# Moving the weight folds, one context split and one normalisation in a cross-attention kernel

## The reference

```
Q = (x @ Wq), K = (ctx @ Wk), V = (ctx @ Wv)      # x: 8 x 256 x 256, ctx: 8 x 256 x 192
score = Q K^T / sqrt(256), masked by mask_BxS2_if1
attn  = softmax(score)                            # 8 heads of width 256
out   = (attn V) @ Wo + x
return (out - mean(out)) * rsqrt(var(out) + 1e-5) * gamma + beta
```

## Time and profile before

| | |
|---|---|
| time, median of 3 | 321.18 us (321.13 to 321.34) |
| time of the profiled execution | 321.24 us |
| its span | 319.4 us |
| PE busy | 309.8 us (97%) |
| DVE, ACT, POOL busy | 253.2, 222.2, 181.0 us |
| granted TensorE clock | 0.998 of full speed |

### The profile page before, as it was taken

One profiled execution on the slowest core, in us unless ns is written; L12 is line 12 of the kernel. 1 busy time (PEld: TensorE's weight loads), 2 busy tenths in 40 slices (PEclk: granted clock), 3 DMA queues, 4 the chain that ended last, 5 costly groups with the idle time before them and its releaser, 6 DMA issues.

```text
span 319.4 us, 7403 instructions
## 1 busy us (share of the span) xinstructions
PE 309.8 (97%) x2264; PEld 290.2 (91%) x2264; DVE 253.2 (79%) x721; ACT 222.2 (70%) x601; POOL 181.0 (57%) x183
## 2 busy tenths in 40 slices
PE   8899998999999999999999999999999999999992
PEld 6898877999999999999999999999999999999982
DVE  0367768777999879987998879987998889975785
ACT  2446677677877787678776887678767887777640
POOL 1123259555864587457864586458755686457211
PEclk9999999999999999999999999999999999999999
DMA  7995444454345653474445454464355445440100
GB/s 257 366 406 213 135 131 129 126 182 136 130 150 166 207 163 113 158 209 168 131 123 179 165 164 143 140 218 149 114 188 163 170 117 182 141 145 13 35 33 33
DMA packets 46910, 50.26 MB, mean 157 GB/s; under 512 B 3504, under 2 KB 37040, under 8 KB 46896
## 3 DMA queue, kind: packets, MB, share of 16 engines
q1 hardware_dynamic: 46608, 49.56, 46.4%
q10 hardware_dynamic: 288, 0.52, 0.6%
HBM read 32.24 MB, written 17.83 MB: 157 GB/s over the span
## 4 chain that ended last, share of the span: by engine, by line
PE 89%; DVE 3%; POOL 2%; DMA 2%; ACT 1%; issue 1%; SPq 1%; POOLq 0%; DVEq 0%
PE score_bank L314 24%; PE out_bank L314 18%; PE gL_bank L314 13%; PE tL_bank L314 12%; PE tU_bank L314 8%; PE gU_bank L314 7%; DMA wq_raw<-in_wqT 2%; PE tL_bank L348 1%; PE spare_bank L348 1%; PE tL_bank L330 1%; PE tU_bank L330 1%; POOL pT_lo L1018 1%; DVE tU L817 1%; PE tU_bank L354 1%; PE spare_bank L314 1%
## 5 line engine op out<-in xcount | busy, mean ns | idle before, releaser
L995 POOL TENSOR_TENSOR probs<-probs,inv_sum 128x512 f32<-128x512 f32 x64 | 66.6, 1042 | 84.5 <-DVE inv_sum L780 83.9
L592 ACT ACTIVATE probs<-neg_scores,neg_max 128x256 f32<-128x256 f32 x128 | 64.2, 502 | 34.7 <-DVE neg_max L769 34.6
L1018 POOL TENSOR_TENSOR pT_lo<-pT_raw,pT_hi 128x512 fp32r<-128x512 f32 x60 | 76.5, 1296 | 11.7 <-ACT pT_hi L549 11.7
L769 DVE CUSTOM_DVE_ANT_0 neg_scores<-score_bank,mask_bias 128x256 f32<-128x256 f32 x128 | 49.1, 421 | 7.4 <-PE score_bank L314 4.6
L790 DVE STREAM_TRANSPOSE squares<-probs 128x512 f32<-128x512 f32 x60 | 42.3, 706 | 0.8 <-DMA scratch<-squares 0.3
L549 ACT ACTIVATE tL_hi<-tL_bank 128x512 fp32r<-128x512 f32 x31 | 18.5, 598 | 30.9 <-PE tL_bank L314 30.9
L314 PE MATMUL score_bank<-ctxT_hi,gU 128*128 128x256 f32 x128 | 36.6, 286 | 0.7 <-POOL ctxT_lo L1007 0.7
L314 PE MATMUL score_bank<-ctxT_hi,gL_lo 128*128 128x256 f32 x128 | 36.3, 284 | 0.0
L314 PE MATMUL score_bank<-ctxT_lo,gL_hi 128*128 128x256 f32 x128 | 36.3, 283 | 0.0
L314 PE MATMUL score_bank<-ctxT_hi,gL_hi 128*128 128x256 f32 x128 | 36.3, 283 | 0.0
L314 PE MATMUL score_bank<-ctxT_lo,gU 128*128 128x256 f32 x128 | 36.2, 283 | 0.0
(11 more groups left out here) (166 smaller groups left out, 946.4 us busy)
## 6 DMA issues: line engine op xcount, KB each, us to landing
scratch<-squares SPq DMA_DIRECT2D x30, 512.0 KB, 2.8
pT_raw<-scratch SPq DMA_DIRECT2D x120, 128.0 KB, 3.1
xT_raw<-in_xT SPq DMA_DIRECT2D x8, 256.0 KB, 4.5
ctxT_raw<-in_ctxT SPq DMA_DIRECT2D x8, 256.0 KB, 4.7
wo_raw<-in_wo SPq DMA_DIRECT2D x4, 512.0 KB, 13.4
x_res<-in_x SPq DMA_DIRECT2D x8, 256.0 KB, 3.2
out<-y_out SPq DMA_DIRECT2D x7, 256.0 KB, 2.7
wq_raw<-in_wqT SPq DMA_DIRECT2D x3, 512.0 KB, 7.9
```

The lines of the kernel that those rows point to most:

```text
L592: nc.scalar.activation(probs[j % 2][:, n, :], neg_scores[:, n, :], ACT.Exp, bias=neg_max[:, n:n + 1], scale=-1.0, accum_out=row_sum[:, n:n ...
L769: nc.vector.tensor_tensor_reduce(out=neg_scores[:, n, :], in0=score_bank[hh][:, q, :], in1=mask_bias[:], scale=-SCALE, scalar=3.0e38, op0= ...
L995: nc.gpsimd.tensor_tensor(probs[j % 2][:, rows, :], probs[j % 2][:, rows, :], inv, ALU.mult) \
L1018: nc.gpsimd.tensor_tensor(pT_lo[j % 2][:, k].rearrange("p hh (q i r) -> p (hh q) i r", q=QT, i=ROWS), pT_raw[j % 2][:, k].rearrange("p i n ...
```

## The change

1. **Folds of C.** Pair t is folded in step t, for t = 0 to 3. On PE a fold now stands ahead of `context_products`, so in step 3 pair 3 is folded ahead of the context products of step 0. The banks become spare/out for pairs 0 and 3 and tL/tU for pairs 1 and 2, on all three engines (`fold_C_banks`); pair 2 waits for the split of pair 1, pair 3 for that of pair 0. Context products of step 0 wait for the splits of three pairs, output products of step 0 for all four.
2. **ACT.** `C_hi_part` moves behind `pT_hi_part` within its step.
3. **Context of batch 0.** `ctx_hi_part(0)` and `ctx_lo_part(0)` move from step 3 to step 1, on ACT behind the query parts, on POOL behind `normalise_probs`.
4. **DVE.** `C_lo_part` stays at the end of the step: pairs 0 to 3 in steps 0 to 3. The wait for gamma and beta moves from ahead of step 3 to ahead of step 4.
5. **Tail.** `normalise(B - 2)` moves behind the last split. Batch 7 is normalised into `y_last`, which is `neg_scores`, and DVE no longer waits for the store of batch 6 there.

```diff
+        y_last = neg_scores[:, 0:QT, :]
+        def fold_C_banks(j):
+            n = (0, 1, 1, 0)[j]
+            return fold_banks[2 * n], fold_banks[2 * n + 1]
...
-                sp.dma_start(out[B - 1][:, q, :], y_out[:, q, :]).then_inc(out_stored, 16)
+                sp.dma_start(out[B - 1][:, q, :], y_last[:, q, :]).then_inc(out_stored, 16)
...
@@ fold_C (PE) @@
-                    pe.wait_ge(C_split, 2 * (j - 2) + 2)
-                lower, upper = fold_banks[2 * (j % 2)], fold_banks[2 * (j % 2) + 1]
+                    pe.wait_ge(C_split, 2 * (PAIRS - 1 - j) + 2)
+                lower, upper = fold_C_banks(j)
...
@@ context_products (PE), j == 0 @@
-                    pe.wait_ge(C_split, 2 * PAIRS)
+                    pe.wait_ge(C_split, 2 * (PAIRS - 1))
...
@@ output_lower (PE) @@
+                if j == 0:
+                    pe.wait_ge(C_split, 2 * PAIRS)
...
@@ step (PE) @@
+                for pair in folds:
+                    fold_C(pair)
                 if not (isinstance(t, int) and t < LAG):
                     context_products(t - LAG, jb, bb)
-                for pair in folds:
-                    fold_C(pair)
...
@@ all engines with folds (PE, ACT, DVE) @@
-            step(0, 0, 0, folds=[0])
-            step(1, 1, 0, folds=[1])
-            step(2, 2, 0, folds=[2, 3])
-            for t in range(LAG, PAIRS + 2):
+            for t in range(PAIRS):
+                step(t, t, 0, folds=[t])
+            for t in range(PAIRS, PAIRS + 2):
...
@@ step (ACT) @@
-                if j == PAIRS - 1:
+                if j == PAIRS - 1 and not (isinstance(t, int) and t < PAIRS):
                     ctx_hi_part(b)
...
+                if isinstance(t, int) and t == 1:
+                    ctx_hi_part(b)
+                if not (isinstance(t, int) and t < LAG - 1):
+                    pT_hi_part(t - LAG + 1, (j - LAG + 1) % PAIRS)
                 for pair in folds:
                     C_hi_part(pair)
-                if not (isinstance(t, int) and t < LAG - 1):
-                    pT_hi_part(t - LAG + 1, (j - LAG + 1) % PAIRS)
...
@@ step (POOL) @@
-                if j == PAIRS - 1:
+                if j == PAIRS - 1 and not (isinstance(t, int) and t < PAIRS):
                     ctx_lo_part(b)
                 normalise_probs(t, j)
+                if isinstance(t, int) and t == 1:
+                    ctx_lo_part(b)
...
@@ tail (DVE) @@
             centre(B - 2)
-            normalise(B - 2)
             t_lo_part_lower(STEPS - 2)
             tU_sum(STEPS - 2)
             t_lo_part_upper(STEPS - 2)
             tU_sum(STEPS - 1)
             t_lo_part_lower(STEPS - 1)
             t_lo_part_upper(STEPS - 1)
+            normalise(B - 2)
...
-            dve.wait_ge(out_stored, 16 * B)
             for q in range(QT):
                 dve.wait_ge(rstd_done, B + q)
-                normalise_tile(B - 1, q)
+                normalise_tile(B - 1, q, y_last)
```

More of the change, by code:

```diff
@@ L846, in centre_tile, with normalise_tile @@
                     ALU.subtract, ALU.mult).then_inc(y_scaled_done, 1)
-            def normalise_tile(b, q):
+            def normalise_tile(b, q, into):
                 dve.wait_ge(y_scaled_done, QT * b + q + 1)
                 nc.vector.scalar_tensor_tensor(
-                    y_out[:, q, :], y_scaled[:, q, :], rstd[:, q:q + 1], beta_sb[:],
+                    into[:, q, :], y_scaled[:, q, :], rstd[:, q:q + 1], beta_sb[:],
                     ALU.mult, ALU.add).then_inc(y_out_done, 1)
@@ L866, in normalise @@
                 for q in range(QT):
-                    normalise_tile(b, q)
+                    normalise_tile(b, q, y_out)
             def step(t, j, b, ends=None, folds=()):
```

## The result

The changed kernel took 319.27 us (median of 4, 319.08 to 319.54) against 321.23 for the kernel before (4 runs, 321.13 to 321.34): a ratio of 0.994, with a 95% interval of 0.9928 to 0.9952. The forecast was 319.3. The profiled execution took 319.14 us with a span of 317.3, so 2.1 less on both counts than that of before.

The account below looks back on a forecast made before the run. PE, busy 270.12 of 271 us, was taken as the bound, leaving only idle time and block-border losses. Front 1.43 plus tail 0.46 made 1.89; the profiled 321.24 gave 319.35, against the median 319.3 us, range 319.0 to 320.2.

Parts of the forecast that it names:

- PE as the bound: Between 20 and 291 us PE is busy 270.12 of 271, so only its idle time or block-border losses can be gained.
- The front's sum, 1.43: PE from fold 2 to step 5's query products, block by block: those products start at 53.79 against 55.22.
- The choice between 0.88 and 1.43: Front gain: 0.88 if only idle times the timeline shows go, 1.43 if slower matmuls go too; it took 1.43.
- slower matmuls beside waits: In the front on PE, 0.21 us of the 1.43: second fold in a row 2.94, scores behind the wait 2.50.
- What was late: POOL's queue ahead of ctxT_lo, which ended as scores(4) began at 52.72: late pT_lo(0) and batch 0's context split.
- its timetable: Front's expected times on ACT, DVE and POOL: maxima(3) near 43.8, inv_sum of head 1 at 47.3, ctxT_lo ending by 49.9.
- The rooms: Time in hand in the front: ctxT_lo 1.5 us ahead of need at 51.40, gL_lo(4) 1.6 us.
- the rival in which the front gives its gain back: pT_hi(0) ahead of pair 2's high parts on ACT delays maxima(3), bringing another wait: 320.7 us, chance 0.07.
- The transfer rival: ACT waits in step 2 for pT_raw(0) to land; slower if after 44.6, for example 321.6 us; chance 0.04.
- The tail, 0.46: With batch 6's normalising behind the last split, tU(30) through tL_lo(31) come 0.46 us earlier, cutting PE's 0.64 to 0.18.
- The idle time left ahead of y(0): DVE idled 1.09 us there; the moved tiles take 0.79 to 0.88, so 0.2 to 0.3 stays.
- Added work of step 1: POOL's context split, about 1.2 us, beside DVE's last instructions of step 1: cost 0 to 0.3, taken as 0.

Follow-up runs that it names:

- Both partial kernels: The kernel before with only the tail's edit, 320.62 us; and the changed kernel with batch 6 normalised where it was before, 319.67 us.
- three copies of 0.52: The changed kernel with three useless copies on ACT in step 2 ahead of pT_hi(0), into a buffer nobody reads: 319.38 us.
- six: The changed kernel with six useless copies on ACT in step 2 ahead of pT_hi(0): 320.94 us.
- the early copies: The changed kernel with a second buffer for step 31's moved share of tU, so ACT copies it ahead of tU_hi(30): 319.11 us.
- the kernel with the doubled tiles: The changed kernel with batch 6's two normalised tiles computed twice behind the last split, first into an unread part of neg_scores: 319.74 us.

## Why the prediction was right

**PE as the bound.** The steps between the two places took what they took before to 0.04 us; nothing was given back in 250 us. Both partial kernels show it, since their parts add.

**The front's sum, 1.43, measured 1.38.** Block by block in the trace after: fold 2.84 (2.84), scores and query products 4.55 (4.53), fold 3 2.83 (2.84), context products 2.40 (2.37), scores 2.40 (2.39). The choice between 0.88 and 1.43, that the slower matmuls go too, was right to 0.05. Of the 0.21 that the prediction calls slower matmuls beside waits, 0.11 is the first matmul behind a wait; the other 0.10 is the second fold in a row, which no wait stands beside, and why it is slower was not tried. (The 0.34 of waits in that sentence is 0.35 by the rows; the gain of 1.43 doesn't hang on it.)

**What was late.** The prediction gave the change two things to take from POOL's queue, the context split and the late pT_lo(0), and left open how the gain divides. The experiments do: with one fold a step the whole gain is there whatever is done with the context split; with the context split alone it is 0.31. ACT's new order brings nothing either. Of the front's three edits one carries it, as far as each was put back alone. The list of two things was also short by one: with pT_lo(0) on time or not, POOL has to wait for the sums of step 3. The prediction has these sums in its timetable (47.3, measured 47.04) but not among what was late.

**The rooms.** For ctxT_lo 1.5 was forecast and 1.6 read; three copies of 0.52 just used it up and cost 0.13, six cost 1.65. So the rival in which the front gives its gain back names a real mechanism, in the form it has there: pair 2's high parts late on ACT, and maxima(3) held behind their split on DVE. It sets in beyond 1.6 us of lateness. The transfer rival would have used the same way, by holding ACT, but the transfer had landed 4 us before ACT asked.

**The tail, 0.46, measured 0.43 to 0.44.** The prediction read the gain off PE's gap, which was to fall from 0.64 to 0.18 and fell to 0.25; 0.04 came from elsewhere in the stretch. The chain through tU(30), tU_hi(30), the copies, tU(31) and tL_lo(31) is as it was written down, since the early copies shorten it. The idle time left ahead of y(0), 0.2 to 0.3, is 0.30 in the list and 0.39 as room.

**Added work of step 1.** Taken as nothing, and nothing it is: DVE's split of pair 1 keeps its place 3.1 us ahead of fold 2 (35.44 on DVE for 38.56 on PE).

**The port pair.** mask_bias of batch 1 took 0.27 us in the trace after (47.12), where it started ahead of POOL's product (47.29), and 0.60 before, where it started behind one. That is again what the Trainium skill, SBUF — State Buffer, "two separate sides", says of the pair that DVE and POOL share: who starts first has it. The two traces fit that with 0.33 us lost in the one case and nothing in the other. It moved nothing on PE's path.

**Median.** That 319.27 meets the 319.29 worked out is in part luck: the parts of the change make 1.38 + 0.43 = 1.81 where the prediction had 1.89, and the medians differ by 1.96. What makes up the rest of the 1.96 was not worked out; the start alone differs by up to 0.38 us between these traces (fold 2 at 38.44 to 38.82).

## What to carry to other kernels

Where one engine is dense for nearly the whole span, look for the few places where it isn't, and follow each back to the queue that is late; a large block that PE can do anywhere (here a weight fold) is best placed where it lets the next long chain start earlier, and not only where its own data are ready. Price a chain by starts, not by the idle times that a list shows: here the first matmul behind a wait cost 0.11 us more, and the room ahead of y(0) was 0.39 where the list showed 0.30. Look for every strand that ends in the late instruction: here taking work from POOL's queue freed 0.3 of 1.4 us, since the sums were late as well. Parts that come with the part that gains, like the context split and the separate buffer here, may do nothing: one experiment each tells.

## What the runs showed of the hardware

**The clock can fall at the start.** The long execution of the kernel with the doubled tiles lost its 2 us ahead of fold 2, which started at 40.70. PE had idled 1.92 us for the load of wq_raw, was at work again from 9.57, and from about 11 on the granted clock stood at 0.50, the lower of the two levels, 1.2 GHz, for some 3 us (in these rows the clock is the third number from the end, ahead of DMA share and GB/s):

```profile
10.00:11.00 1.00, 1.00 (x7) 1.00 (x7) 0.00 (x0) 0.00 (x0) 0.10 (x1) 0.96 1.02 414
11.00:12.00 1.00, 1.00 (x5) 1.00 (x5) 0.15 (x1) 0.55 (x2) 0.00 (x0) 0.50 1.04 421
...
13.00:14.00 1.00, 1.00 (x5) 1.00 (x4) 0.00 (x0) 0.18 (x1) 0.00 (x0) 0.50 1.02 357
14.00:16.00 2.00, 2.00 (x13) 2.00 (x12) 0.62 (x2) 0.92 (x4) 0.00 (x0) 0.92 0.92 306
```

The fold at 11.02 took 2.76 us there, against 1.46 in the other traces. From the end of the wait to the fold that starts at 15.25 it was 5.68, where the kernel before took 13.37 - 9.36 = 4.01. Before the change PE had idled 1.86 at the same place, and its clock did not fall. No other profiled execution shows it. What decides between the two was not tried.

**The first matmul behind a wait.** It lasts 0.39 us in place of 0.28 (128x256, at 52.72 before), and the next one starts 0.11 later than in a dense stream. The same shows without idle time where the block behind a fold begins (0.39 at 41.40 above).

**Landing times.** Stores of the squares landed late now and then and held DVE, at another place in each trace: for 0.38 us in step 2 with the context split put back, for 0.35 at 58.38 before, for 0.20 at 179.19 after, for 0.48 at 144.50 with the early copies. The first of them showed on PE's path. Single executions of the changed kernel differ by up to 0.46 us (319.08 to 319.54), more than the smallest edit here is worth; how much of that is such a store and how much the start was not measured.
